# A masked gather that comes out of the matrix product already turned

## The reference, cut to what matters

```python
k = int(CAP * s)                                   # 64
topv, topi = jax.lax.top_k(weights, k)
kc = k - 1                                         # 63 chosen tokens
sel_idx = jnp.sort(topi[:, :kc], axis=1)
...
m = attention_mask[:, 0]                           # [4, 512, 512]
m_sel = m[bidx[:, :, None], sel_idx[:, :, None], sel_idx[:, None, :]]
...
sc = jnp.einsum('bhqd,bhkd->bhqk', q, kk) / np.sqrt(hd).astype(np.float32)
sc = sc + m_sel[:, None]
a = jax.nn.softmax(sc, axis=-1)
```

## Time and profile before

| | |
|---|---|
| device time, three runs | 831.65, 833.54, 834.04 us; median 833.54 |
| span of the profiled execution | 830.0 us (its own device time is not listed apart; the median is 3.54 us above the span) |
| instructions | 16995 |
| busy: TensorE, VectorE, ScalarE, GpSimd | 82%, 72%, 67%, 47% of the span |
| TensorE weight loads | 48% |
| mean granted TensorE clock | 0.828 of full speed |
| SP's transfers | 36.75 MB, mean 44 GB/s |

### The profile page before, as it was taken

The page is one execution under the profiler, slowest core; times in us unless marked ns, Lnnn a source line. Parts: engine busy times, 40 slices in busy tenths (PEclk is TensorE's granted clock), DMA queues, the critical chain, the costliest instruction groups (busy, mean ns, idle before and its releaser), DMA issues.

```text
span 830.0 us, 16995 instructions
## 1 busy us (share of the span) xinstructions
PE 678.9 (82%) x6576; PEld 401.4 (48%) x6576; DVE 595.4 (72%) x1681; ACT 554.2 (67%) x403; POOL 392.0 (47%) x399
## 2 busy tenths in 40 slices
PE   3588787889979988999899988998899879865652
PEld 2344334455546455645455545645565535434232
DVE  4442718777787788958888788769896986588455
ACT  0588688889768876959768876788687968600000
POOL 5263436447544574346455664446546543421201
PEclk8567678899789987989789987899799979985755
DMA  6321302033300503030304030120303030000001
GB/s 190 64 42 37 64 13 53 25 61 119 64 14 17 112 12 67 27 64 14 64 14 90 14 64 15 50 54 2 64 26 65 2 64 27 13 1 26 0 0 51
DMA packets 96913, 36.75 MB, mean 44 GB/s; under 512 B 68018, under 2 KB 94146, under 8 KB 96834
## 3 DMA queue, kind: packets, MB, share of 16 engines
q1 hardware_dynamic: 96834, 35.67, 18.8%
HBM read 14.69 MB, written 4.19 MB: 23 GB/s over the span
## 4 chain that ended last, share of the span: by engine, by line
PE 61%; DVE 18%; issue 10%; ACT 7%; POOL 3%; DMA 1%; POOLq 0%; DVEq 0%; ACTq 0%
PE ps_y L1199 16%; PE ps_s L1182 14%; ACT pr L731 4%; PE ps_m L1308 3%; PE ps_m L1230 3%; ACT th L716 3%; PE ps_m L1206 3%; PE ps_a L1230 3%; PE ps_m L1356 2%; PE ps_a L1393 2%; DVE v_aug L844 2%; PE ps_m L1258 2%; PE ps_a L1206 2%; PE ps_a L1258 1%; PE ps_a L1292 1%
## 5 line engine op out<-in xcount | busy, mean ns | idle before, releaser
L716 ACT ACTIVATE th<-ps_s 128x1024 f32<-128x1024 f32 (+1 forms) x256 | 280.2, 1129 | 110.7 <-PE ps_s L1182 102.0
L627 POOL TENSOR_TENSOR pr<-pr,tri 128x320 f32<-128x320 f32 (+1 forms) x256 | 194.8, 784 | 186.7 <-ACT pr L731 186.7
L731 ACT ACTIVATE pr<-th 128x2304 f32<-128x2304 f32 x128 | 271.5, 2122 | 15.5 <-PE ps_y L1199 15.4
L1182 PE MATMUL ps_s<-q_st,k_st 32*64 32x512 f16 (+7 forms) x2048 | 193.1, 319 | 24.9 <-ACT th L716 20.8
L1199 PE MATMUL ps_y<-pr,v_aug 128*32 128x512 f32 (+7 forms) x2048 | 157.4, 439 | 0.4 <-POOL pr L627 0.4
L1182 PEld LDWEIGHTS ps_s<-q_st,k_st 32*64 32x64 f16 x2048 | 92.3, 114 | 120.0 <-issue 54.3
L1199 PEld LDWEIGHTS ps_y<-pr,v_aug 128*32 128x32 f32 x2048 | 57.0, 113 | 66.9 <-issue 47.4
L641 POOL TENSOR_TENSOR st<-qk,st 128x1024 f16<-128x1024 f32 x32 | 73.8, 2327 | 32.3 <-DVE st L860 32.3
L629 POOL TENSOR_TENSOR k_wide<-qkT,head_of 128x1024 f32<-128x1024 f32 x16 | 30.1, 1902 | 58.0 <-DVE qkT L1029 58.0
L629 POOL TENSOR_TENSOR r<-x,rw_row 128x512 f32<-128x512 f32 x16 | 18.9, 1180 | 63.6 <-DVE x L922 63.6
L702 ACT ACTIVATE hq<-hu 128x512 f32<-128x512 f32 x8 | 5.0, 630 | 60.7 <-POOL hu L629 60.7
(11 more groups left out here) (220 smaller groups left out, 1133.9 us busy)
## 6 DMA issues: line engine op xcount, KB each, us to landing
x_in<-in_L_attn_x SPq DMA_DIRECT2D x16, 256.0 KB, 2.8
x_res<-in_L_attn_x SPq DMA_DIRECT2D x16, 256.0 KB, 3.1
result<-y_out SPq DMA_DIRECT2D x16, 256.0 KB, 2.4
mask_a<-in_L_ffn_attention_mask SPq DMA_DIRECT2D x3, 1024.0 KB, 5.2
pr<-in_L_ffn_attention_mask SPq DMA_DIRECT2D x2, 1024.0 KB, 8.6
w_sb<-in_L_ffn_w SPq DMA_DIRECT2D x2, 256.0 KB
q_st<-st SPq DMA_TRANSPOSE x16, 4.5
k_st<-st SPq DMA_TRANSPOSE x16, 4.7
```

The source lines that it names most:

```text
L627: return nc.gpsimd.tensor_tensor(buf, buf, tri[:, None, :].to_broadcast([P, blocks, 64]), ALU.mult)
L716: nc.scalar.activation(th[:, gi % 2, c0:c1], ps_s[:, c0:c1], ACT.Tanh, scale=1.0 / (QK_SCALE ** 2 * DH ** 0.5 * SOFTCAP))\
L731: nc.scalar.activation(pr[:, probs_at(n):probs_at(n) + GROUP], th[:, gi % 2, :], ACT.Exp, scale=SOFTCAP).then_inc(exp_done, 1)
L1182: last = mm(ps_s[64 * s:64 * s + 64, COL[kb]:COL[kb] + S - 64 * kb], k_st[rows, k, gi // 2, 64 * kb:64 * kb + 64], q_st[rows, k, gi // 2, ...
```

## The change

The product is made the other way round: blocks of the mask, 128 x 128, are the stationary operand, and E's columns stream past them. The result is already the turned one. `sel.R` with its copy and its four transposes is gone; `sel.RT` is now 16 products of 128 columns a pair where both sequences share the mask (pairs 2 to 7), and 32 products of 64 columns where they do not (pairs 0 and 1). The first two column blocks are in slot 29 ahead of `sel.qkT`, the other two in slot 30. The waits of SP, of ScalarE and of the PSUM bank that were on `R` are on `RT`.

```diff
-    ["sel.qkv@-1", "pv.3/1@0"], ["sel.R@-1", "sel.R1@-1", "sel.R2@-1", "sel.R3@-1", "sel.qkT@-1"],
-    ["sel.RT@-1"], ["prep.xT/1@1", "sel.msel@-1"],
+    ["sel.qkv@-1", "pv.3/1@0"], ["sel.RT0@-1", "sel.RT1@-1", "sel.qkT@-1"],
+    ["sel.RT2@-1", "sel.RT3@-1"], ["prep.xT/1@1", "sel.msel@-1"],
...
-    ["fin.root1/0@0", "fin.root2/0@0", "sel.R@-1", "sel.qkT@-1", "fin.yU0/1@0"], ["sel.RT@-1", "prep.xT/1@1"],
+    ["fin.root1/0@0", "fin.root2/0@0", "sel.qkT@-1", "fin.yU0/1@0"], ["sel.RT@-1", "prep.xT/1@1"],
...
-                    pe["sel"].wait(sp, p - 1, "R")
+                    pe["sel"].wait(sp, p - 1, "RT")
...
-                            pe["sel"].wait(act, 1, "R")
+                            pe["sel"].wait(act, 1, "RT")
...
-                if k == 0:
-                    pe["sel"].wait(v, b.pair - 1, "RT")
...
-            sel_R = copy_step("sel", "R", lambda: nc.vector.tensor_copy(R[:, :], at("sel.R")[:, :]),
-                              [(ve["route"], lambda q: Batch(q, 1), f"win{NT - 1}")])
...
-            def sel_R(q, c):
-                if c == 0:
-                    bank_free("sel.R", q)
+            def sel_RT(q, j):
+                if j == 0:
+                    bank_free("sel.RT", q)
                     t_.wait_ge(mask_loaded, {0: 32, 1: 64}.get(q, 80))
-                for k in range(2):
-                    last = mm(at("sel.R")[SLOTS * k:SLOTS * k + SLOTS, :], E[:, c, SLOTS * k:SLOTS * k + SLOTS],
-                              (mask_b if k and q < 2 else mask_a)[:, c, :], start=(c == 0), stop=(c == NT - 1),
-                              skip_group_check=True)
-                if c == NT - 1:
-                    pe["sel"].done(last, "R", q)
-
-            def sel_RT(q, _):
-                ve["sel"].wait(t_, q, "R")
-                bank_free("sel.RT", q)
-                four(at("sel.RT"), lambda c: R[:, P * c:P * c + P], pe["sel"], "RT", q)
+                shared = ((mask_a, 0, P),) if q >= 2 else ((mask_a, 0, SLOTS), (mask_b, SLOTS, P))
+                for mask, lo, hi in shared:
+                    for c in range(NT):
+                        last = mm(at("sel.RT")[:, P * j + lo:P * j + hi], mask[:, c, P * j:P * j + P], E[:, c, lo:hi],
+                                  start=(c == 0), stop=(c == NT - 1), skip_group_check=True)
+                if j == NT - 1:
+                    pe["sel"].done(last, "RT", q)
```

More of the change, by code:

```diff
@@ L81 @@
     "sel": ["xs", "ss"] + rsqrt_of("r1", 1) + rsqrt_of("r1", 2) +
-        ["hn", "ET", "hnT", "cosp", "sin0", "sin1", "rope", "vv0", "vv1", "R", "qkT", "RT", "msel"],
+        ["hn", "ET", "hnT", "cosp", "sin0", "sin1", "rope", "vv0", "vv1", "qkT", "RT", "msel"],
     "att": ["sc0", "mx0", "sub0", "sc1", "mx1", "sub1", "den", "rden", "PT0", "PT1", "o0", "o1", "oT", "x1f",
@@ L91 @@
     "route": ["wrow", "won", "thr"],
-    "sel": ["gather", "ET", "hnT", "qkv", "R", "qkT", "RT", "msel"],
+    "sel": ["gather", "ET", "hnT", "qkv", "qkT", "RT", "msel"],
     "att": ["S0", "S1", "P0T", "P1T", "PV", "oT", "wo", "h2T", "w1"],
@@ L222 @@
     "sel.ET": "m",
-    "sel.R": "m",
     "sel.RT": "m",
@@ L267 @@
     "sel.ET": ["fin.yT/0@1", "late.z1@-1"],
-    "sel.R": ["sel.hnT@0"],
-    "sel.RT": ["sel.R@0"],
+    "sel.RT": ["sel.hnT@0"],
     "sel.gather": ["fin.y1/0@1", "route.rank/1@0"],
@@ L406, in build @@
         ET = sb("ET", [P, S])
-        R = w_wide
         RT = sb("RT", [P, NT, P])
@@ L1135, in _ @@
                      "route.row": route_row, "route.win": route_win, "route.rank": route_rank, "route.coef": route_coef,
-                     "sel.xs": sel_gather, "sel.ET": sel_ET, "sel.R": sel_R, "sel.ss": sel_squares, "sel.hn": sel_hn,
+                     "sel.xs": sel_gather, "sel.ET": sel_ET,  "sel.ss": sel_squares, "sel.hn": sel_hn,
                      "sel.RT": sel_RT, "sel.hnT": sel_hnT, "sel.qkv": sel_qkv, "sel.msel": sel_msel,
@@ L1416, in _ @@
                      "fin.yT": fin_yT, "fin.wo": fin_wo, "route.wrow": route_wrow, "route.won": route_won, "route.thr": route_thr, "sel.gather": lambda q, _: sel_gather(q, 0), "sel.gather1": lambda q, _: sel_gather(q, 1),
-                     "sel.ET": sel_ET, **{f"sel.R{c or ''}": (lambda q, _, c=c: sel_R(q, c)) for c in range(NT)}, "sel.RT": sel_RT, "sel.hnT": sel_hnT, "sel.qkv": sel_qkv,
+                     "sel.ET": sel_ET, **{f"sel.RT{j}": (lambda q, _, j=j: sel_RT(q, j)) for j in range(NT)}, "sel.hnT": sel_hnT, "sel.qkv": sel_qkv,
                      "sel.msel": sel_msel, "sel.qkT": sel_qkT, "att.S0": lambda q, _: att_scores(q, 0),
```

## The result

The changed kernel is slower by about 1%: 841.04 us median of 4 runs (838.24 to 848.57) against 833.7 (831.65 to 834.04); the ratio is 1.0108, 95% interval 1.0068 to 1.0148. The forecast was 834.9, no measurable change, in a range of 829.0 to 840.0. Ratios leave out runs more than 1.5% above the fastest of their kernel (here none, in e3 eight of twelve, in e15 one of four), while medians and ranges are of all runs.

A forecast was written before the change was run, and what follows sets the result against it. TensorE was taken as the bound in pairs 0 to 5, a serial chain over VectorE and GpSimd in pairs 6 and 7. +6.5 - 1.4 - 1.9 - 1.8 = +1.4 us on 830.0, plus 3.5 to the median: 834.9 us, range 829.0 to 840.0.

The forecast's parts named there:

- Pairs 0 and 1, +6.5 us: TensorE's product there: 64 instructions of 64 columns at 0.11 us, 7.4 us against 4.17, +3.2 a pair.
- Rival 1: Pairs 0 and 1: weight loads no longer hidden, 0.165 us an instruction, +6.7 a pair, 841.8 us in all; chance 0.12.
- Pairs 2 to 5, -1.4 us: TensorE's product there: 32 instructions of 128 columns, 3.8 us against 4.17 for R and its transposes, -0.35 a pair.
- Rival 2: All pairs: TensorE streams small products quicker than 0.11 us, at 0.08, giving 826.3 us; chance 0.05 with its nearer form.
- Rival 2's lesser form: Pairs 0 and 1 alone at 0.055 us an instruction: 3.8 us there, 829.1 in all; shares the chance of 0.05.
- Rival 5: Pairs 2 to 5: the small gains do not arrive, an equal wait opens behind msel, 836.3 us; chance 0.10.
- Rival 3: Pairs 0 and 1: ScalarE holds the pace, falling back by 2.0 us, not 3.2; 832.5 us in all; chance 0.13.
- Pairs 6 and 7, -3.7 us: Transposes of q and k come earlier, so GpSimd and the second layer's scores do: -1.9 us in pair 6, -1.8 in pair 7.
- rival 4: Pair 7: second layer's scores start before the clock falls, one or both halves save 0.9 us, 833 to 834; chance 0.12.
- At nothing: SP's load of the masks: SP's load of the next masks, issued at 188.93, comes about 5 us later at no cost; masks needed a pair later.
- At nothing: the split of the product: Product over two slots: score unit behind the first block comes earlier, behind the second by 0.35 us; no cost counted.
- The sum: Whole kernel: +6.5 - 1.4 - 1.9 - 1.8 = +1.4 us on the span of 830.0; 834.9 us as median.

The follow-up runs named there:

- e3: The changed kernel run again without any change, for its spread: 847.64 us (833.18 to 850.39, 12 runs).
- e15: The changed kernel with twelve more products (2.7 us) in pair 0: 844.52 us, ratio 1.0113.
- e6: The kernel before with one step of R (0.85 us) issued once more in pair 0: 838.85 us, ratio 1.0067.
- e2: The changed kernel with the old way back in pairs 2 to 7, so new in pairs 0 and 1 alone: 845.52 us, ratio 1.0139.
- e5: The changed kernel with the old way back in pairs 0 to 5, so new in pairs 6 and 7 alone: 829.61 us, ratio 0.9983.
- e8: e1 with two products more (0.44 us) in each of pairs 2 to 5: 834.54 us, ratio 1.0025.
- e1: The changed kernel with the old way back in pairs 0 and 1, so new in pairs 2 to 7: 832.08 us, ratio 1.0001.
- e4: The kernel before with R's whole product issued twice in pairs 0 and 1: 841.56 us, ratio 1.0109.
- e13: The changed kernel with four more products (0.9 us) in pair 0: 846.56 us, ratio 1.0163.
- e11: e5 with only one column block of the new product ahead of the transposes of q and k: 828.54 us, ratio 0.9944.
- e10: e5 with a product with V moved into TensorE's gap ahead of `late.sc1`: 862.69 us, ratio 1.0332.

## Why the prediction was wrong, by its own steps

- **Pairs 0 and 1, +6.5 us: right.** 2 x 3.71 us against the 7.4 of the text, +3.12 a pair instead of +3.2. A load of 128 x 128 float32 weights hides 64 columns as it hides 32. Rival 1 is excluded: 0.111 us an instruction, not 0.165. That the measured 841.04 lies beside its 841.8 is chance.
- **Pairs 2 to 5, -1.4 us: right for the product**, -0.36 each instead of -0.35, and its instructions start one after another (16 in 1.98 us). In the profiled execution pair 4 did not keep the gain: +1.0 us, with the wait for `k_st`. Rival 2, and with it the 81 ns of the Trainium skill ("TensorE: Matmul & The Clock Gate", "Back-to-back issue gap"), does not hold for this float32 product: sixteen in 1.86 us of loads. Rival 2's lesser form was also summed wrongly: 3.8 us in pairs 0 and 1 with the -1.4 of pairs 2 to 5 gives 827.7, not 829.1, which is below the range. Rival 5, a wait that eats the gain, came true in one pair of four, at the score unit behind the first block and not behind `sel.msel`.
- **Rival 3: its mechanism was there, without its effect.** ScalarE did wait in pair 0's stretch, 1.95 us for a score unit, as worked out (2.0), in ScalarE's timeline:

```profile
191.35 1.02 ACT L713 ACTIVATE th<-ps_s 128x1024 f32<-128x1024 f32 x1
194.32 1.24 ACT L713 ACTIVATE th<-ps_s 128x1280 f32<-128x1280 f32 x1 [1.95 <-PE ps_s L1175]
```

  But TensorE's marks moved by the full 3.12, so TensorE, not ScalarE, held the pace.
- **Pairs 6 and 7, -3.7 us: right in sum, -3.6**, not in parts. GpSimd started 1.5 us earlier in each, 3.26 and 4.39 after the product's start, not 1.9 and 1.8. In pair 6 VectorE was busy with a norm's small steps when the transposes were ready, work that the text had not looked for between them; in pair 7 the first block lay wholly at half clock. What that lost, the scores of pair 7 at full clock gave back (1.08 for 1.97), as rival 4 had it.
- **At nothing: SP's load of the masks right.** It was issued at 193.65 instead of 188.93, and the turning transfer at 222.34 instead of 219.13, with the shift of everything; the trace has no wait for either.
- **At nothing: the split of the product, wrong in pair 4.** The text has the score unit behind the first block "earlier", and did not ask whether its keys are there by then. They were not, once in four pairs: 1.3 us of the span.
- **The sum: wrong.** The step that failed is the last sentence of rival 4, "the levels may as well fall otherwise elsewhere, by as much", which priced the clock over the whole run at 0.9 us either way, and the sum took it at nothing. In the profiled execution the stretches with the same instructions took 3.9 us more, at 6.8 us more of half clock, and the wait above another 1.3; by the medians the local sum is missed by 6.1 us (841.04 against 834.9). The changed kernel's 16 runs lie between the local sum (833.8) and 17 us above it. A local delay is not only its own length: everything behind it meets the clock at another moment. The runs of the kernel before gave no warning, since they are within 2.4 us. The trace did: iterations 3 and 5 pass units 24 to 27 in 13.6 us and the others in 10 to 11, for the same instructions.
- **A smaller error:** the 3.5 us between span and median were carried over as if they were fixed. The changed kernel's profiled run took 838.24 with a span of 836.4, so 1.8 lay around the span. In the runs of before 1.8 to 3.4 did; with 1.8 its profiled execution, at some 831.8 (an estimate), was one of its shortest.

What is shown: the local costs; that a shift of old work alone can cost 5.6 us beyond its length (e6); that e2's excess lies in stretches of old work; that the long executions are long where more of the clock is at half; and that 1.3 us of the changed kernel's excess in its profiled execution is a wait for `k_st`. What stays open: why the kernel before is so steady (29 of 34 of its runs beside e5 to e8 lie within 3 us, while e1 and e8 spread over 11 to 12), and whether the rest of the excess is position alone or in part the new work of pairs 0 and 1, as the difference of e2 and e4 allows. e8 and e13 to e15 were meant to tell, and did not.

## What to carry to other kernels

Turning a gather so that the wide table is the stationary operand saves a copy and transposes but gives up two things: column groups that run side by side, and a weight load that serves 512 columns. Where two small stationary blocks stream 512 columns two abreast, the turned product is no cheaper, and where it must be split into 64 columns it costs nearly twice (7.4 us for 4.2). It pays at the places where a serial chain waits behind it (here pairs 6 and 7: 4.0 us in e5's profiled execution, 4.5 by e11's median). Where work comes earlier than before, look also for what it reads: a transfer that was hidden before may end the wait now. In a kernel whose TensorE clock falls and rises in every iteration, a change of a few microseconds is measured only with its shift: compare marks between the two traces, split the difference by equal and unequal clock, and add a delay of known size to the kernel before as a control.

## What the runs showed of the hardware

- One program on one core, the same instructions, took 833.2 to 850.4 us (e3), with a mean granted clock of 0.835 and 0.839 in its two shortest runs and 0.822 to 0.830 in the others.
- A delay of 0.85 us early in the run cost 6.5 us in the median; 1.7 us at the same place cost 0.5.
- A float32 product with 128 x 128 weights takes 0.111 us an instruction at full clock with 32, 64 and 128 columns, and 0.21 at half clock.
- One product moved to where it has to wait, ahead of a stretch of small ones, went with a rise of the time at half clock in units 20 to 31 from 17.1 us (e5) to 71.7 (e10) over six iterations.
- A score unit that came 1.75 us earlier waited 1.28 us for a transfer of `k_st` issued 5.9 us ahead of it (the changed kernel); issued 9.8 us ahead, before, it did not wait.
